# Experts computed for chosen rows only, sorted into blocks of 128

## The reference

```python
logits = h @ gate_w.T
scores = jax.nn.softmax(logits.astype(jnp.float32), axis=-1)
topk_w, topk_idx = jax.lax.top_k(scores, K)          # K = 6 of E = 16
cw = jnp.zeros((T, E), jnp.float32)
cw = cw.at[jnp.arange(T)[:, None], topk_idx].add(topk_w)
for e in range(E):
    g = h @ w_gate[e].T
    u = h @ w_up[e].T
    out = jax.nn.silu(g) * u @ w_down[e].T
    y = y + cw[:, e:e + 1].astype(x.dtype) * out
```

## Time and profile before

| | us |
|---|---|
| median of 3 runs | 653.91 |
| lowest and highest | 647.69, 656.65 |
| span of the profiled execution | 653.6 |
| PE busy, share of the span | 593.8, 91% |
| DVE busy | 402.8 |
| ACT busy | 295.4 |
| POOL busy | 167.2 |

### The profile page before, as it was taken

One profiled execution on the slowest core, in us unless ns is written; L12 is line 12 of the kernel. 1 busy time (PEld: TensorE's weight loads), 2 busy tenths in 40 slices (PEclk: granted clock), 3 DMA queues, 4 the chain that ended last, 5 costly groups with the idle time before them and its releaser, 6 DMA issues.

```text
span 653.6 us, 10661 instructions
## 1 busy us (share of the span) xinstructions
PE 593.8 (91%) x3642; PEld 468.5 (72%) x3642; DVE 402.8 (62%) x772; ACT 295.4 (45%) x479; POOL 167.2 (26%) x261
## 2 busy tenths in 40 slices
PE   5889999887888658699999999999999999999995
PEld 4667777663555446588888888888888888888884
DVE  5757877689989635367666555555555555555553
ACT  3585666468879633344444333333333333333331
POOL 6534775938868562000000000000000000000000
PEclk9789999799989857899999999999999999999999
DMA  9700000000000042344543132111231221231211
GB/s 254 254 2 2 1 3 2 1 1 2 1 2 1 1 162 77 87 129 135 141 133 104 59 97 98 65 65 65 64 124 63 64 68 66 82 100 65 64 60 46
DMA packets 37464, 45.90 MB, mean 70 GB/s; under 512 B 10720, under 2 KB 24688, under 8 KB 37296
## 3 DMA queue, kind: packets, MB, share of 16 engines
q1 hardware_dynamic: 34304, 41.19, 20.8%
q0 software_dynamic: 1008, 3.67, 1.7%
q10 hardware_dynamic: 2112, 0.52, 0.4%
HBM read 41.04 MB, written 4.33 MB: 69 GB/s over the span
## 4 chain that ended last, share of the span: by engine, by line
PE 61%; POOL 1%; DVE 1%; ACT 1%; issue 0%; DVEq 0%; POOLq 0%
PE psG L1373 6%; PE psY L1386 6%; PE psG L1375 6%; PE psG L1374 6%; PE psY L1389 6%; PE psU L1375 6%; PE psU L1373 6%; PE psY L1388 6%; PE psU L1374 6%; PE psAux L1314 1%; PE psT L1314 1%; PE psY L1334 1%; PE psT L1399 1%; POOL r_rstd L1280 1%; ACT gw L1500 0%
## 5 line engine op out<-in xcount | busy, mean ns | idle before, releaser
L1472 ACT ACTIVATE act_hi<-x_tok 128x512 fp32r<-128x512 f32 x88 | 55.5, 632 | 161.7 <-DVE x_tok L1601 161.7
L1594 DVE TENSOR_TENSOR x_tok<-psU,x_tok 128x512 f32<-128x512 f32 x88 | 60.8, 691 | 103.3 <-PE psU L1375 103.1
L1605 DVE TENSOR_TENSOR act_lo<-x_tok,act_hi 128x512 fp32r<-128x512 f32 x88 | 60.9, 693 | 62.5 <-ACT act_hi L1472 62.4
L1291 POOL DMA_DIRECT2D out_dram<-x_tok x3 | 2.3, 773 | 300.7 <-DVE x_tok L1612 300.7
L1466 ACT ACTIVATE x_tok<-psG 128x512 f32<-128x512 f32 x88 | 52.7, 600 | 58.4 <-PE psG L1375 58.2
L1386 PE MATMUL psY<-act_hi,wd_lo 128*128 128x512 f32 x176 | 71.1, 404 | 4.9 <-DVE act_lo L1605 4.9
L1373 PE MATMUL psG<-h3T_hi,wg_lo 128*128 (+1 forms) x176 | 69.9, 397 | 0.3 <-DVE logit L1638 0.3
L1389 PE MATMUL psY<-act_hi,wd_hi 128*128 128x512 f32 x176 | 69.2, 393 | 0.0
L1374 PE MATMUL psG<-h3T_lo,wg_hi 128*128 (+1 forms) x176 | 69.1, 392 | 0.0
L1388 PE MATMUL psY<-act_lo,wd_hi 128*128 128x512 f32 x176 | 69.1, 392 | 0.0
L1375 PE MATMUL psG<-h3T_hi,wg_hi 128*128 (+1 forms) x176 | 69.0, 392 | 0.0
(11 more groups left out here) (226 smaller groups left out, 1170.5 us busy)
## 6 DMA issues: line engine op xcount, KB each, us to landing
cw_rows<-cw_spill SPq DMA_DIRECT2D x80, 128.0 KB, 2.9
cw_rows<-cw_spill SPq DMA_DIRECT2D x16, 224.0 KB, 3.0
cw_rows<-cw_spill SPq DMA_DIRECT2D x16, 192.0 KB, 2.7
w_stage<-in_L_ffn_w_gate_dram SPq DMA_DIRECT2D x11, 256.0 KB, 2.8
w_stage<-in_L_ffn_w_up_dram SPq DMA_DIRECT2D x11, 256.0 KB, 2.8
cw_rows<-cw_spill SPq DMA_DIRECT2D x16, 160.0 KB, 2.5
wg_nat<-in_L_attn_w_gate_dram SPq DMA_DIRECT2D x1, 2048.0 KB, 16.4
x_spill<-x_tok SPq DMA_DIRECT2D x1, 2048.0 KB, 7.3
```

The source lines that it names most:

```text
L1472: nc.scalar.activation(a_hi[s % 2][:, :], a[s % 2][:, :], ACT.Copy).then_inc(s_ahi, 1)
L1594: nc.vector.tensor_tensor(a[s % 2][:, :], psU[s % 2][:, :], a[s % 2][:, :], ALU.mult).then_inc(s_t, 1)
L1605: nc.vector.tensor_tensor(a_lo[s % 2][:, :], a[s % 2][:, :], a_hi[s % 2][:, :].bitcast(F32), ALU.subtract).then_inc(s_alo, 1)
```

## The change

The tokens are handled in two parts of 1024. After the choice, each token's row, with its 16 shares and its number (288 values, `hrow`), is written by POOL to six places of a DRAM table (`slots`), one indirect DMA of 128 rows for each tile and choice: 48 a part. The places are computed with small matmuls (`ranks`) and DVE operations (`choice`), so that the rows of one expert lie together and each expert begins at a multiple of 128. A part has 8 x 6 + 15 = 63 blocks (`NTILE`) whatever the choice is; places that nobody takes hold zeros and point at a spare row (`clear_slots`, issued in the attention stage).

Then 126 blocks run in turn. SP loads a block into a ring of 8 (`hin`). PE turns it, reads the offset of its expert's weights from `woff` into a register (`value_load`), and multiplies with the rows stationary and the weights moving: 6 matmuls of 352 columns for gate and up, 5 of 256 for down. DVE finds each row's share for the block's expert (`tile_share`). The block's result goes to one of 3 buffers (`y`) and POOL adds its rows to one of three DRAM tables (`sums`), by an indirect DMA that accumulates. Behind the first 52 blocks 40 of the second part's scatters are mixed in. The three tables of a part, one of which holds x, are loaded, added and stored: the first part's between the blocks of the second, the second part's at the end. The weights of an expert are loaded whole through a ring of 2 (`load_expert`) and all lie in `k.W` before the first block.

```diff
-W_RING = 4
-W_UNITS = [(m, j) for j in range(NCH // 2) for m in range(3)]
...
+PARTS = 2
+PT = NT // PARTS
+PP = NP // PARTS
+NTILE = PT * TOPK + E - 1
+TILES = PARTS * NTILE
...
+RING = 2
+HIN = 8
+SUMS = 3
...
+def load_expert(eng, k, e):
+    r = e % RING
+    for m in range(2):
+        eng.dma_start(k.gu_stage[r][:, m, :], k.expert_w[m][e, 0:P, :]).then_inc(k.gu_loaded[r], 16)
+        eng.dma_start(k.gu_stage[r][0:FE - P, 2 + m, :], k.expert_w[m][e, P:FE, :]).then_inc(k.gu_loaded[r], 16)
+    down = k.expert_w[2][e].rearrange("(c p) f -> p c f", p=P)
+    eng.dma_start(k.d_stage[r][:, :, 0:FE], down).then_inc(k.d_loaded[r], 16)
+    eng.dma_start(k.d_stage[r][:, :, P + 64:P + 64 + FE - P], down[:, :, P:FE]).then_inc(k.d_loaded[r], 16)
...
+def clear_slots(eng, k):
+    for q in range(PARTS):
+        eng.dma_start(k.slots[q].rearrange("(r p) c -> p r c", p=P),
+                      k.pad_row[:, :].unsqueeze(1).to_broadcast([P, NTILE, ROW])).then_inc(k.cleared, 16)
...
+                def tile_rows(t):
+                    q, i = divmod(t, NTILE)
+                    if i == 0:
+                        sp.wait_ge(s_scat[q], 16 * PT * TOPK)
+                    if t == 0:
+                        sp.wait_ge(s_row, NT)
+                        sp.wait_ge(k.x2_spilled, 16 * PARTS)
+                    if t >= HIN:
+                        sp.wait_ge(s_acc[(t - HIN) % SUMS], added(t - HIN))
+                for e in range(RING, E):
+                    sp.wait_ge(s_gu, e - RING + 1)
+                    sp.wait_ge(s_d, e - RING + 1)
+                    load_expert(sp, k, e)
+                for t in range(TILES):
+                    tile_rows(t)
...
+                for a in range(SUMS):
+                    sp.wait_ge(s_acc[a], 16 * TILES // SUMS)
+                for c in range(CHUNKS):
+                    for a in range(SUMS):
+                        sp.dma_start(fin_b(c, a), sum_rows(k, 1, a)[:, 2 * c:2 * c + 2, :]).then_inc(s_fin[c], 16)
...
+                def scatter(q, m):
+                    n, j = q * PT + m // TOPK, m % TOPK
+                    pool.indirect_dma_start(
+                        out=k.slots[q], out_offset=bass.IndirectOffsetOnAxis(ap=slot[:, n, j:j + 1], axis=0),
+                        in_=hrow[:, n, :], in_offset=None, bounds_check=SLOTS - 1, oob_is_err=False
+                    ).then_inc(s_scat[q], 16)
+                def add_rows(t):
+                    q = t // NTILE
+                    pool.wait_ge(s_y, t + 1)
+                    if t >= SUMS:
+                        pool.wait_ge(s_acc[t % SUMS], added(t - SUMS))
+                    pool.indirect_dma_start(
+                        out=k.sums[q][t % SUMS],
+                        out_offset=bass.IndirectOffsetOnAxis(ap=hin[t % HIN][:, ID_COL:ID_COL + 1].bitcast(I32), axis=0),
+                        in_=y[t % SUMS], in_offset=None, compute_op=ALU.add).then_inc(s_acc[t % SUMS], 16)
...
+                for q in range(PARTS):
+                    pool.wait_ge(s_slot, q + 1)
+                    if q == 0:
+                        pool.wait_ge(s_row, PT)
+                        for m in range(total):
+                            scatter(0, m)
+                    else:
+                        for m in range(SECOND_FIRST):
+                            scatter(1, m)
+                        done = SECOND_FIRST
+                pool.wait_ge(k.x2_spilled, 16 * PARTS)
+                for t in range(TILES):
+                    add_rows(t)
+                    while done < total and (done - SECOND_FIRST) * SECOND_UNTIL < (t + 1) * (total - SECOND_FIRST):
+                        scatter(1, done)
+                        done += 1
...
+                pairs(0, PP)
+                gate_up(0)
+                down(0)
+                gate_up(1)
+                ranks(0)
+                for e in range(2, E // 2):
+                    down(e - 1)
+                    gate_up(e)
+                pairs(PP, NP)
+                down(E // 2 - 1)
+                gate_up(E // 2)
+                gate_up(E // 2 + 1)
+                ranks(1)
+                down(E // 2)
+                for e in range(E // 2 + 2, E):
+                    down(e - 1)
+                    gate_up(e)
+                down(E - 1)
...
+                def front(t, off):
+                    pe.wait_ge(s_lo, pairs_done + t + 1)
+                    if t >= 2:
+                        pe.wait_ge(s_a, t - 1)
+                    out = psGU[t % 2]
+                    for c in range(DC):
+                        hi = weights(off, OFF_HI + c * GU, P, GU)
+                        nc.tensor.matmul(out, hT_lo[t % 2][:, c, :], hi, start=(c == 0), stop=False)
+                        nc.tensor.matmul(out, hT_hi[t % 2][:, c, :], weights(off, OFF_LO + c * GU, P, GU),
+                                         start=False, stop=False)
+                        last = nc.tensor.matmul(out, hT_hi[t % 2][:, c, :], hi, start=False, stop=(c == DC - 1))
...
+                def back(t, off):
+                    pe.wait_ge(s_alo, t + 1)
+                    if t >= 2:
...
+                for s in range(TILES + 2):
+                    if s < TILES:
+                        offs[s] = pe.value_load(woff[0:1, s:s + 1], min_val=0, max_val=(E - 1) * WS)
+                        front(s, offs[s])
+                    if 0 <= s - 1 < TILES:
+                        act_turned(s - 1)
+                    if s >= 2:
+                        back(s - 2, offs[s - 2])
+                    if s + 2 < TILES:
+                        tile_turned(s + 2)
...
+                def product_out(t):
+                    act.wait_ge(s_G2, t + 1)
+                    if t >= SUMS:
+                        act.wait_ge(s_acc[t % SUMS], added(t - SUMS))
+                    nc.scalar.activation(y[t % SUMS], psY[t % 2], ACT.Copy).then_inc(s_y, 1)
...
+                def product(t):
+                    dve.wait_ge(s_sg, t + 1)
+                    dve.wait_ge(s_share, t + 1)
+                    if t >= 2:
+                        dve.wait_ge(s_T2, t - 1)
+                    up, gate = psGU[t % 2][:, FE:GU], sg[t % 2]
+                    by = share[:, t % 4:t % 4 + 1]
+                    nc.vector.scalar_tensor_tensor(out=act_buf[:, t % 2, 0:P], in0=up[:, 0:P], scalar=by,
+                                                   in1=gate[:, 0:P], op0=ALU.mult, op1=ALU.mult)
...
+                for s in range(TILES + 2):
+                    if s + 1 < TILES:
+                        tile_share(s + 1)
+                    if s < TILES:
+                        product(s)
+                    if 0 <= s - 1 < TILES:
+                        act_low(s - 1)
+                    if s + 2 < TILES:
+                        tile_low(s + 2)
```

More of the change, by code:

```diff
@@ L1403, in turn, with pairs @@
[L1403 to L1408 removed]
+                def pairs(first, end):
+                    for i in range(first, end + 1):
+                        if i < end:
+                            rows(i)
+                        if i > first:
+                            logits(i - 1)
+                            logits_out(i - 1)
@@ L1662, in _ @@
-                with dve.Fori(1, NG) as g:
-                    for s in range(NCH):
-                        n = g * NCH + s
-                        product(n, s)
-                        shared(g, s)
-                        low(n, s)
-                        if s in (1, 2):
-                            output(g - 1, s - 1)
-                for half in range(2):
-                    output(NG - 1, half)
+                pairs(0, PP)
+                choice(0)
+                gate_up_low(0)
```

857 lines of the change are left out of this document (452 added, 405 removed).

## The result

| | before | after |
|---|---|---|
| median of 4 runs | 653.2 us (647.7 to 656.7) | 713.7 us (709.1 to 717.0) |
| ratio | | 1.094, 95% interval 1.087 to 1.101 |
| span of the profiled execution | 653.6 us | 711.1 us |

A forecast was written before the change was run, and what follows sets the result against it. PE's matmul stream was taken to bound the old kernel; in the new one POOL paces 52 blocks, then PE. Entry 335 + 52 x 2.30 + 73 x 2.21 + end 26 = 642, stated as 641 us; range 612 to 745.

The forecast's parts named there:

- POOL at 1.2 + 0.1 us for every indirect DMA: First 52 blocks: 92 indirect DMAs at 1.3 us set 2.30 us a block, over PE's 2.21.
- both marks of my own rival (1.42 and 1.5): POOL's us per indirect DMA at which its chain passes the time before (1.42) and the 2% slower mark (1.5).
- POOL sets the pace: Rival: POOL's indirect DMAs bound the kernel and make it slower, 725 us, chance 0.20.
- The rival's own formula: POOL's chain as a time: 444 + 148x us, x being us from one indirect DMA to the next.
- PE's beat, 2.21: Block loop: PE's matmuls and transposes take 2.08 us a block, plus two waits on register operations at 0.07 each.
- The offset load at nothing: Block loop: PE's load of a block's weight offset is covered by its queue's lead and adds 0 us.
- the rival that had it exposed: Rival: the offset load takes over 0.95 us and shows, beat 2.5 to 2.8, time 690 us, chance 0.12.
- The first part's tables at nothing: Block loop: the sum has no term for loading and adding the first part's tables between the second part's blocks.
- The entry: From 233.3 us: tile pairs, choices and experts' weights at 3.2 us an expert; first block's `front` ends at 335.
- The rings don't bind: Block loop: `y` needs 4.6 us per 3 blocks and `hin` allows a beat of 2.0, so neither sets the pace.
- The clearing DMAs are hidden, the end is 26: Eight clearing DMAs take 90 us from about 50 us, hidden before 233.3; last `front` to kernel end takes 26 us.
- The other two rivals: Adds land late, at 6 us: 700 us, chance 0.06. Clock falls to 1.2 GHz: over 850 us, chance 0.02.

The follow-up runs named there:

- experiment 1: Changed kernel without the 40 second-part scatters that stand between the first 52 blocks: 685.3 us, against 713.7.
- experiment 2: Changed kernel with the blocks' 126 indirect DMAs writing their rows instead of adding them: 673.2 us, against 713.7.
- experiment 4: Changed kernel with the fourth matmul of the second product on all 128 rows instead of 64: 698.1 us, against 713.7.
- experiment 9: Nine row buffers instead of eight, against the kernel with the 128-row matmul and without the second part's 40 scatters between blocks (669.7 us): 653.3 us.
- experiment 3: Changed kernel with fixed weight addresses, no offset load or register offsets on PE: 708.3 us; with the load put back but unused: 711.2 us; against 713.7.
- experiment 5: Changed kernel with the first part's eight table additions moved from POOL to DVE: 709.2 us, against 713.7.
- experiment 10: Changed kernel plus 128-row matmul, DVE table additions, sorted transposes: 695.9 us; then second part's choice earlier, more scatters ahead: 670.9; table loads spread: 669.7; ninth row buffer: 655.8.
- experiment 6: Changed kernel with each expert's entry transposes sorted, four of 128 rows before four of 48, not in turns: 705.0 us, against 713.7.

## Why the prediction was wrong

The predicted sum was 335 + 281 + 26 = 642. Measured, in the same terms (end of the first `front`, end of the last, end of the kernel): 350.1 + 335.5 + 25.5 = 711.1.

- **Which step failed: POOL at 1.2 + 0.1 us for every indirect DMA.** The upper bound in the text, 1.6, held, but I took one price for two kinds. A scatter was near it, 1.00 + 0.30; an adding DMA costs 1.54 + 0.30. The mean over the mixture, (52 x 1.84 + 40 x 1.33) / 92 = 1.62, is past both marks of my own rival (1.42 and 1.5), so by its rule "POOL sets the pace", with chance 0.20, was the case that happened. The rival's own formula gives 684 at 1.62, and its case stood at 725: the rest of the way to 711 is in the points below. POOL set the pace in half the loop only: 57 distances at 2.82 in place of 2.30, 30 us (shown by experiments 1 and 2). Behind them 1.84 lies under PE's beat.
- **PE's beat, 2.21.** Measured 2.38, from a cause that is no term of the sum: one matmul of 64 rows, worth 0.33 us of the beat (experiments 4 and 9). I had priced all five of `back` by columns, 5 x 0.12, and added two bumps at waits, 0.14, for register operations that cost nothing (experiment 3). Without the 64 rows the sum of columns and transposes, 2.08, is right: 2.05 measured.
- **The offset load at nothing** was right, and the rival that had it exposed is refuted: 2.38 with and without.
- **The first part's tables at nothing.** Twelve loads and eight additions in the loop had no price in my sum. Blocks 69 to 97 came at 2.78: 12 us over the undisturbed beat. Some 3 of them are this execution's own, with the clock at half for 3.4 us; POOL's additions are about 3 more (experiment 5); with these gone and the loads spread, a ninth buffer for the rows took off 6 (experiment 10). How the rest divides is open.
- **The entry**, 15 us too short. The choice ended at 261.0, as predicted to within 2 us. An expert took 4.2 us in the first part and 3.9 in the second, and not 3.2, which is about 10 of the 15: the change of rows in every transpose, which the sum didn't have, and right behind it the ring of two (experiment 6). The sum had each four pairs at a price between those of the two clocks, and the second part's ran at the low one, 13.5 us for 12. The rest lies in waits between these pieces, and what the half clock adds to an expert stays open.
- **The rings don't bind.** Right at 2.38, and wrong for the beat that I had forecast: I put the ring of rows at 2.0 with 1.2 on POOL and 3 us for the landing. With the measured 1.54 + 0.30, a landing 3.9 after that and 2.6 for the load the same working gives (0.7 + 1.84 + 3.9 + 2.6) / 4 = 2.26, over 2.21. At 2.06 it cost 16 us (experiment 9).
- **The clearing DMAs are hidden, the end is 26**: both right. The clearing DMAs had landed before 100 us, the attention stage and the choice ended where they should, and the end took 25.5.
- **The other two rivals** didn't happen: the additions landed after 3.9 us (median) and not 6, and the clock fell in the loop in four stretches of 3.4 us only, which cost 1.4 us at the 58th distance and some 3 in blocks 69 to 97.

Added up: 15 in the entry, 30 in the first 57 distances, 1.5 at the 58th, 29 x (2.78 - 2.21) = 16.5 in blocks 69 to 97 (5 of them for the beat), 6.5 for the beat in the other 38, less 0.5 at the end, are the 69 us between 642 and the profiled 711.1.

## What to carry to other kernels

Work that is halved in columns is not halved in time when it is cut into blocks: each block brings its own POOL DMAs, its own small waits and its own round trip through a ring, and the engine that had nothing to do (POOL, 26% busy) can become the one that sets the pace. Count each engine's work per block by kind, from the start of one instruction to the next and not by its busy time, and price a DMA that adds apart from one that only writes. A ring that is "just enough" at one beat binds at the next faster one: after each gain, work out its latency again.

## What the runs showed of the hardware

- An indirect DMA of 128 rows holds POOL 0.96 to 1.03 us, one that adds 1.54 us; 0.30 us follow either. They land 3.0 and 3.9 us after issue (medians).
- A matmul of 64 rows between ones of 128 costs 0.38 us at its place at full clock; transposes of 128 and 48 rows in turns cost 2.7 us for eight at half clock, sorted 1.6.
- A register load from SBUF takes PE's queue 307 ns (median), register offsets 42 to 46 ns each; neither showed in the beat. The Trainium skill (page "DMA: Bandwidth & Descriptors", section "Latency and other measured facts") has a floor of about 600 ns for such a load; here the measurement decides.
- A DVE operation of 16 columns with two SBUF inputs, 0.23 us elsewhere, took 1.93 to 2.56 us beside each of eight POOL additions of 1.84 us, and ended with them.
- Among fp32 transposes, with two bf16 matmuls of 512 columns for each expert between them, the granted clock stayed at 0.50 though PE was busy 22.97 of 23 us.
